# LayerNorm statistics of the first router and the sine layer: within the attentions, or in the stages that use them

## The reference

```
x += tanh(g) * concat_linear(ln(x), mean(ctx))            L0 attention's place
x += tanh(g) * quantised_ffn(ln(x))                       L0
x += tanh(g) * attention_16_heads(ln(x), ctx)             L1   ("l1x")
x += tanh(g) * mixture_of_experts_top_2_of_8(ln(x))       L1   ("l1f", the first router)
x += tanh(g) * attention_with_normed_q_k(ln(x), ctx)      L2   ("l2x")
x += tanh(g) * sine_ffn(ln(x))                            L2   ("l2f", the sine layer)
x += tanh(g) * masked_attention(ln(x), ctx)               L3   ("l3x")
x += tanh(g) * token_choice_experts(ln(x))                L3   ("l3f")
ln(x) = (x - mean(x)) / sqrt(var(x) + 1e-5)               over the 128 features of a token
```

## Time and profile before

| | |
|---|---|
| median of 3 runs | 1387.22 us (1386.28 to 1392.21) |
| the profiled execution | 1392.32 us |
| its span, first to last instruction | 1390.3 us |
| busy in the span | PE 1096.1, PE's weight loads 799.3, DVE 883.0, ACT 776.0, POOL 825.9 us |
| mean granted TensorE clock | 0.896 |
| first attention, about | 218 to 356 us |
| first router, its score part | 356 to 384 us |
| second attention | 682 to 818 us |
| sine layer | 818 to 925 us |

### The profile page before, as it was taken

One profiled execution on the slowest core, in us unless ns is written; L12 is line 12 of the kernel. 1 busy time (PEld: TensorE's weight loads), 2 busy tenths in 40 slices (PEclk: granted clock), 3 DMA queues, 4 the chain that ended last, 5 costly groups with the idle time before them and its releaser, 6 DMA issues. The chain is left out here.

```text
span 1390.3 us, 26343 instructions
## 1 busy us (share of the span) xinstructions
PE 1096.1 (79%) x8968; PEld 799.3 (57%) x8968; DVE 883.0 (64%) x2026; ACT 776.0 (56%) x1506; POOL 825.9 (59%) x1207
## 2 busy tenths in 40 slices
PE   5682487998627999865699877879997895999993
PEld 5431374666526999655466644647775653666662
DVE  6789976999371111256599968969996587334331
ACT  3378466888544454355488866648887542233220
POOL 5300235888406555388277769738887555588875
PEclk9696689999758999988799989989998896999997
DMA  3000000110026888522011110001110113455542
GB/s 118 9 0 0 6 14 7 20 20 16 5 68 179 250 235 225 138 63 58 8 19 21 20 25 13 1 3 17 21 21 17 77 39 116 97 106 113 98 87 23
DMA packets 99222, 82.57 MB, mean 59 GB/s; under 512 B 54697, under 2 KB 78130, under 8 KB 98834
## 3 DMA queue, kind: packets, MB, share of 16 engines
q1 hardware_dynamic: 83282, 62.65, 16.0%
q0 software_dynamic: 15808, 18.24, 8.1%
HBM read 57.15 MB, written 16.12 MB: 53 GB/s over the span
## 5 line engine op out<-in xcount | busy, mean ns | idle before, releaser
L1726 PE MATMUL ps<-topk_up_sb,topk_wu 128*128 128x512 f32 x256 | 122.6, 616 | 0.7 <-issue 0.7
L1527 POOL DMA_INDIRECT out<-topk_shared,l3f_route_slots x64 | 102.5, 1601 | 20.4 <-issue 14.6
L1614 ACT ACTIVATE topk_ga<-ps 128x512 f32<-128x512 f32 x64 | 38.6, 602 | 125.0 <-PE ps L1726 125.0
L2203 ACT ACTIVATE l1f_g_h<-ps,l1f_g_wd 128x256 f32<-128x256 f32 x156 | 62.7, 474 | 73.0 <-DMA l1f_g_wd<-l1f_W 49.2
L1870 DVE TENSOR_TENSOR sb_xnT<-topk_ga,ps 128x512 f32<-128x512 f32 x64 | 44.1, 688 | 92.5 <-ACT topk_ga L1614 91.5
L2233 DVE TENSOR_TENSOR l1f_g_y<-ps,l1f_g_wd 128x256 f32<-128x256 f32 x39 | 16.6, 425 | 134.6 <-PE ps L2176 134.6
L2112 POOL DMA_INDIRECT l1f_g_xg<-l1f_rows,l1f_route_slots x78 | 75.0, 961 | 17.7 <-issue 12.5
L2167 PE MATMUL ps<-l1f_g_xgT,l1f_g_wu 128*128 128x256 f32 x312 | 75.6, 386 | 1.7 <-ACT l1f_g_xgT L2195 0.9
L2176 PE MATMUL ps<-l1f_g_wd,l1f_g_h 128*128 128x128 f32 x624 | 75.9, 276 | 0.0
L1523 POOL DMA_INDIRECT topk_xg<-l3f_rows,l3f_route_slots x64 | 62.7, 979 | 19.7 <-issue 17.7
L2176 PEld LDWEIGHTS ps<-l1f_g_wd,l1f_g_h 128*128 128x128 f32 x624 | 72.8, 192 | 0.0
(11 more groups left out here) (515 smaller groups left out, 3445.1 us busy)
## 6 DMA issues: line engine op xcount, KB each, us to landing
l1f_g_wd<-l1f_W SPq DMA_DIRECT2D x39, 322.0 KB, 4.0
l1f_g_wu<-l1f_W SPq DMA_DIRECT2D x39, 256.0 KB, 3.9
topk_wu<-l3f_W SPq DMA_DIRECT2D x16, 512.0 KB, 4.0
l1f_y_rows<-l1f_g_y SPq DMA_DIRECT2D x39, 128.0 KB, 4.0
topk_wd<-l3f_W SPq DMA_DIRECT2D x16, 256.0 KB, 2.8
l3f_rows<-l3f_route_own_rows SPq DMA_DIRECT2D x1, 2304.0 KB
sb_x<-x SPq DMA_DIRECT2D x8, 256.0 KB, 6.3
sb_l0f_up<-sb_l0f_up SPq DMA_DIRECT2D x128, 9.6 KB
```

The source lines that it names most:

```text
L1527: pool.indirect_dma_start(out=out_rows, out_offset=spot(g, i), in_=y[g % 2][:, i, :], in_offset=None, compute_op=ALU.add).then_inc(y_added ...
L1726: ins = pe.matmul(ps[:, 2 * (c % 2) + i, :], wu[g % W][:, (i * CX + c) * P:(i * CX + c + 1) * P], xgT[g % 2][:], start=True, stop=True)
L2203: sc.activation(h[g % 2][:, c, :], ps[:, c, 0:GS], ACT.Gelu, bias=wd[g % W][:, C * P + c:C * P + c + 1]).then_inc(acted, 1)
```

## The change

The attentions l1x and l2x no longer take the statistics; l3x still does. The norms of the first router and of the sine layer are no longer `ready`, so they get tables of their own (`st` and `mv`, 768 and 256 bytes a partition), their `stats` calls do the work, where they always stood in DVE's order, and their roots on ACT wait for the bn_aggr of the chunk. The last layer's router keeps `ready`. Nothing else moves.

```diff
--- before.py
+++ after.py
@@ -477,7 +477,7 @@
         sp.dma_start(t["vpad"][j % 2][row:row + many, c, :, 32 * i:32 * i + 32], src[:, :, 32 * i:32 * i + 32]).then_inc(came, 16)
 
 
-def attention(nc, t, d, layer, gate_at, bias_v=False, bias_out=False, masked=False):
+def attention(nc, t, d, layer, gate_at, bias_v=False, bias_out=False, masked=False, stats=True):
 
 
 
@@ -759,11 +759,11 @@
             for k in range(NT + 3):
                 if k + 1 < NT:
                     raw_weights(k + 1)
-                if k >= 3:
+                if stats and k >= 3:
                     spread(k - 3)
                 if k < NT:
                     total(k)
-                if k >= 3:
+                if stats and k >= 3:
                     joined(k - 3)
                 if k < NT:
                     invert(k)
@@ -1159,7 +1159,7 @@
     with ExitStack() as ctx:
         s = Sems(nc, ctx, stage + "r")
         rows = t["own_rows"]
-        ln = Norm(nc, ctx, t, stage + "r", s, lambda n: rows[:, n, 0:D], ("pool", "pool", "pool", "dve" if norm else "act"), ring=False, ready=True)
+        ln = Norm(nc, ctx, t, stage + "r", s, lambda n: rows[:, n, 0:D], ("pool", "pool", "pool", "dve" if norm else "act"), ring=False, ready=not norm)
         shared_here = s.one("shared_here")
         loads, steps, sq_ready, norm_ready, vec_ready, vec_turned, vec_kept, both_made, both_kept = (
             s.one("loads"), s.one("steps"), s.one("sq_ready"), s.one("norm_ready"), s.one("vec_ready"), s.one("vec_turned"),
@@ -2532,7 +2532,7 @@
     UP = 5
     with ExitStack() as ctx:
         s = Sems(nc, ctx, stage)
-        norm = Norm(nc, ctx, t, stage, s, two_blocks(t["stage"]), ("pool", "pool", "pool", "pool"), bank=5, banks=1, ready=True)
+        norm = Norm(nc, ctx, t, stage, s, two_blocks(t["stage"]), ("pool", "pool", "pool", "pool"), bank=5, banks=1)
         after = Norm(nc, ctx, t, stage + "_after", Sems(nc, ctx, stage + "_after"), lambda n: t["xc"][:, n * P:(n + 1) * P], ("pool", "pool", "act", "dve"),
                      ring=False, chunks=(5 * TB, TB, TB, TB), rows=t["row_any"])
         q_made, q_kept = s.one("q_made"), s.one("q_kept")
@@ -2837,7 +2837,7 @@
                 u = dict(t)
                 u["kT"], u["vall"] = keys_and_values(own, layer)
                 prepare(u)
-                attention(nc, u, d, layer, gate_at, **k)
+                attention(nc, u, d, layer, gate_at, stats=False, **k)
 
         def token_choice():
 
@@ -2897,7 +2897,7 @@
                 if 1 in stages:
                     quantised_ffn(nc, u, d, 4, "l1x")
             if 2 in stages:
-                attention(nc, u, d, "l1x", 1, bias_v=True, bias_out=True)
+                attention(nc, u, d, "l1x", 1, bias_v=True, bias_out=True, stats=False)
         with ExitStack() as held:
             t["maskall"] = held.enter_context(nc.sbuf_tensor("l3x_maskall", [P, NT * KEYS], BF16))
             if 3 in stages:
```

## The result

| | kernel before | kernel after |
|---|---|---|
| median of the first comparison | 1389.72 us (1386.28 to 1392.58, 4 runs) | 1407.18 us (1405.71 to 1414.06, 4 runs) |
| ratio, 95% interval | | 1.0118 (1.0092 to 1.0144) |
| profiled execution; its span | 1392.32; 1390.3 us | 1405.71; 1403.6 us |

The changed kernel is slower by 1.2%, +16.4 us (12.8 to 20.0) by the ratio and +17.5 us by the two medians of four runs. The forecast was +13.4 us, a ratio of 1.0097; that lies in the interval, and the difference of the two spans is 13.3 us. But the time named was 1400.6 us with a range up to 1406.0, and 1407.18 is outside it. Two things are to be explained: where the 13 us are, and where the other 3.

A forecast was written before the change was run, and what follows sets the result against it. The prediction took ACT, at 3.88 us a tile, to bound the attentions, not DVE. Its terms, -1.1 + 0 + 6.5 + 8.0 = +13.4 us on the median of 1387.2, gave 1400.6 us, range 1393.4 to 1406.

The forecast's parts named there:

- Steady part of the attentions: Both attentions' steady tiles: dropping statistics gains 0, as ACT's 3.88 us sets the tile; gain at most 2.5 us.
- The first rival (DVE as the bound): Attentions: DVE sets the tile, which falls to 3.61 us, -16.2 us in all, kernel 1384.4 us; chance 0.04.
- The two tails, -1.1: End of both attentions: the last bn_aggr behind POOL's last add goes, 0.54 us twice, -1.1 us.
- Router, +6.5: First router: five chunks of statistics on DVE delay the last root by 6.5 to 6.6 us; bounds +4.5 to +8.5.
- items 2 and 3: First router, statistics of chunks 1 and 2, the latter ahead of the copy at L1302: +0.8 and +1.5 us.
- Item 6: First router behind the last root: PE has run ahead, -0.8 us, against +0.8 for TensorE's lower clock lasting longer.
- The +0.8 for a clock that stays low longer: First router: new holes let TensorE's granted clock stay longer at 0.50, the lower level (1.2 GHz), +0.8 us.
- this rule: Trainium skill on TensorE's clock: throttled by default, activity releases it; alone, it has the clock fall in every statistics hole.
- Sine layer, +8.0: Sine layer's start: chunks 2 to 4 in series delay the last root, +8.9 - 0.2 - 0.7 us; bounds +7.0 and +9.0.
- The -0.7 us for a fuller start of the loop: Sine layer's first block: PE has five matmuls ready and POOL starts without holes, -0.7 us.
- The rival of a half caught up start: Router or sine layer: late starts partly caught up, half of 14.5 us left, +6.2 us, 1393.4 us; chance 0.13.
- the forecast's own upper bound of +16.4: Whole kernel: upper bounds of the terms, -1.1 for the attentions, +8.5 router, +9.0 sine layer, +16.4 us.

The follow-up runs named there:

- stages_twice: Against the kernel before: attentions keep their statistics, the first router and sine layer take them once more; 1.0116 (1.0094 to 1.0139), +16.2 us.

## Why the prediction was right and wrong

- **Steady part of the attentions, 0:** right. The median tile got no shorter without the statistics, nor longer with twice as many. The first rival (DVE as the bound) is out. One of my reasons was thin: the 0.18 us that DVE waited for POOL's fold was the only such wait in 110 us.
- **The two tails, -1.1:** right. From the start of POOL's last add to the next stage's first instruction it is 1.88 or 1.89 us for every attention that takes the statistics once, in all traces, and 1.36 to 1.39 for every one that does not (2.23 with two sets): 0.5 us each. The whole lengths of the attentions gain only 0.6 us in the mean, but they spread by 1 us and more.
- **Router, +6.5:** the five chunks' arithmetic came out nearly as written: the copy at L1302 is 2.0 us late (2.3 by items 2 and 3) and the last root 6.5. (The items as listed add to 6.6.) Item 6 was mis-sized: I cancelled -0.8 against +0.8, and only the first came. Of the 1.2 us for which ACT still waited for PE behind the last root, the stage got 1.1 back, so that it is 5.4 us longer in the first pair of traces and 5.6 in the mean. The +0.8 for a clock that stays low longer came from no row. The clock did stay low longer (0.59 from 371 to 376 us, 0.81 before), but ACT was late enough not to notice, except for 1 us in stages_twice; nor did it fall in every hole, for it was 1.00 from 376 to 381 us, with PE busy for 3.6 of the 5. My sentence that without this rule the item would be 0 is wrong too: the item stood at 0 with it, and would have been -0.8.
- **Behind the router:** I let nothing happen there, without a reason; +1.0 us was seen, of unknown cause.
- **Sine layer, +8.0:** the first angle was to be late by 8.9 - 0.2 and is by 9.1. The -0.7 us for a fuller start of the loop was wrong: the loop gives back 0.1 (73.0 us against 73.1). The term should have been 0, which makes the sum +8.7; measured are +8.9 to +9.0. The rival of a half caught up start is out.
- **The sum:** +13.4 forecast, +14.9 by stages, +16.4 by the ratios. The stages differ from the terms by -0.9 us (router), +1.0 (behind it), +0.9 (sine layer) and +0.5 (attentions), which partly cancel; the last 1.5 us of the ratios stay open. That +13.4 met the 13.3 us between the first two spans is in part luck.
- **The step that failed** is the last one, from the sum to a time and a range. I set +13.4 on 1387.22 us, the median of three runs, though the profiled execution against which every term was worked out took 1392.32. The measured median lies 6.6 us over the time named: 2.5 of it is the base, which a fourth run moved to 1389.72, and 4.1 is the change, +17.5 by medians against +13.4. In the later comparisons on chips of the same speed the kernel before has medians of 1392.64 and 1392.43 (17 runs each). 1387.22 was low, and the profiled execution stood for the kernel. The profiled time that I gave for the changed kernel, 1405.7, is what its profile measured, 1405.71; that is luck in part, since this execution was the fastest of four, up to 1414.06. And the top of the range, 1406.0, took in bounds of the change but not the 5 us by which single runs of one kernel differ, which I quoted and then left out; the forecast's own upper bound of +16.4 on 1392.32 would have reached 1408.7.

## What to carry to other kernels

Work taken off an engine with a 94% busy share was worth nothing here, where another engine sets the tile: look for the engine that never waits outside a fixed round trip, and count gaps that no wait explains as room. Work moved from a steady loop into the start of a stage is paid nearly in full once the waits for the stage's loads are used up (the first chunks hid there), because the rest stands ahead of everything else. If it must be there, take it back to back, beside loads and table loads, and not in chunks with a round trip each (9.1 us against 3.4 for the same tiles here). Put a forecast on the same footing as its terms: if they come from one profiled execution, set the sum on its time and widen the range by the spread of the runs.

## What was not expected of the hardware

- The same program took 1392 us on two of the chips and 1435 and 1441 on two others, with the router and the sine layer's start and loop alike to 0.3 us and the attentions to 0.7. Most of the difference lies in one stretch, from the first gathered row of the combine (L2296) to the second attention's first maximum, 101 to 102 us on the former and 128 to 140 on the latter; it holds 64 indirect loads, but which of its waits grew was not traced. The stretch from L1790 to the first indirect transfer of the output (L1527) took 96 to 97 us and 103 to 110. The ratios agree between the two kinds of chip within their intervals.
- 28 matmuls of no use ahead of the router brought TensorE from 1.2 to 2.4 GHz and made the stage 1.3 to 2.1 us shorter. With the late statistics of the changed kernel behind them, the granted clock was back at 0.55 some 15 us into the stage, and the stage gained 0.2 us.
- The granted clock falls at different places in runs of one program, and a tail of 25.2 us at 1.00 becomes 29.7 us at 0.83.
